# Feed-forward of a two-layer block in fp32: product and masked product stay in the PSUM bank of up, VectorE takes the low part from there, GpSimd only splits weights

## The chip, the cores and the metric

The kernel runs on one core of one Trainium2 chip. The metric is the device time of one execution in microseconds (us), lower is better. All times here are of that one core.

## The reference

The input x is 4 x 512 tokens of 128 numbers. It goes through two layers, each an alignment or attention step followed by a feed-forward. Only the feed-forwards matter here; each is a mixture of experts behind a layer norm.

```python
# layer 0: 64 experts of 64 hidden rows, 8 chosen for each token, and one shared expert
gate_out = jnp.einsum('bsh,ehi->bsei', hidden_states, expert_gate_k)
up_out = jnp.einsum('bsh,ehi->bsei', hidden_states, expert_up_k)
expert_act = jax.nn.silu(gate_out) * up_out
routed = jnp.einsum('bsei,eih->bsh', expert_act * router_mask[..., None], expert_down_k)
return shared + routed
...
# layer 1: 8 experts of 344 hidden rows, 2 chosen for each token, and one shared expert
for e in range(E):
    y = y + cw[:, e:e + 1] * _ffn(xf, wg[e], wu[e], wd[e])     # _ffn: silu(x wg') * (x wu') wd'
y = y + _ffn(x, swg, swu, swd)
```

router_mask and cw are zero for the experts that a token did not choose. The kernel computes all experts for all tokens and multiplies by the mask.

## The kernel before, in words

**Arithmetic.** A matmul in fp32r keeps fewer bits than fp32. So each factor is split into a high part (a copy rounded to fp32r) and a low part (the number less its high part), and a product is three matmuls into one PSUM bank: high x high, low weight x high, high weight x low (`three_pass`, L1010 to L1014).

**Tiling.** The hidden rows of all experts are cut into groups of 128: 33 in the first feed-forward, 25 in the second. The 2048 tokens are four chunks of 512. A group and a chunk are a unit: 132 units, then 100. `feed_forward(f)` stands in the program of each engine; f is 0 or 1, g the group, k the chunk, u = 4g + k the unit, i = k % 2 the buffer.

**One unit.**
- TensorE, `gate_up` (L1128): gate into bank 4 or 5, up into bank 6 or 7, three matmuls of 128x512 each (L1012 to L1014).
- ScalarE, `unit` (L836): silu of the bank of gate into act_s (L846).
- VectorE, `unit` (L1629): product act_t = act_s x bank of up (L1639), then the masked product act_a = act_t x mask (L1647).
- ScalarE, `hi` (L829): high part act_hi of act_a (L834).
- GpSimd, `unit` (L695): low part act_lo = act_a - act_hi (L700).
- TensorE, `down` (L1141): three matmuls into the bank of the chunk, 0 to 3 (L1144, L1145, L1147), which adds up over all groups.

**Order.** It is written by hand, with a semaphore for each step. TensorE does gate and up of unit u and then down of unit u-2; ScalarE silu of u, then the high part of u-1. Everything between is double buffered: act_s, act_t, act_a, act_hi, act_lo and the banks 4/5 and 6/7. The first three groups (PEEL) and the last two (REST) are unrolled; the rest is a loop over four groups (BODY).

**Waits around the change.** Gate of unit u waits for silu and for the product of unit u-2, which is what frees the bank of up:

```python
pe.wait_ge(FF[f]["silu"], u - 1)
pe.wait_ge(FF[f]["t"], u - 1)
```

The masked product waits for the low part of u-2 (the reader of act_a). The high part and the low part wait for down of u-2, which frees act_hi and act_lo.

**Weights.** SyncE loads w_raw a group ahead; ScalarE copies it to w_hi (L842) at chunk 2 of the group before; VectorE then makes w_lo (`split_lo`, L1623 to L1627). The splits of groups 0 and 1 are made earlier, by `first_lo`. Masks come by DMA from scr_mask, two for each group.

**Ends.** Before unit 2, TensorE starts the banks 0 to 3 with matmuls of one row of zeros (L1173). In the first units of the second feed-forward VectorE also does the routing of layer 1 (`route1`, L1468), in pieces ahead of units 0 to 3.

## Time and profile before

| | |
|---|---|
| runs | 926.32, 926.35, 929.34 us, median 926.35 |
| span of the profiled execution | 928.2 us |
| TensorE matmuls | 714.0 us busy, 77% |
| VectorE | 773.9 us busy, 83% |
| ScalarE | 432.5 us busy, 47% |
| GpSimd | 438.0 us busy, 47% |

The profile is of one execution. Its span runs from the first to the last instruction; what a run has around it is small, as the three runs lie from 1.9 us below that span to 1.1 us above it. In the rows, PE is TensorE's matmuls, PEld its weight loads, DVE VectorE, ACT ScalarE, POOL GpSimd. Names are those of the program without buffer numbers: "bank" is any PSUM bank, "arena" is the SBUF area that holds mask, act_s, act_t and act_a. L12 is line 12 of the kernel before. The records of two matmuls in a row overlap, so their starts tell the pace. Waits name the engine that waited and the last one that released it.

### The profile page before, as it was taken

To read this page: it belongs to the slowest core of one execution; us is meant where nothing else is said; L and a number is where in the kernel's file an instruction comes from. 1 tells how busy PE (TensorE), PEld (TensorE's weight loads), DVE (VectorE), ACT (ScalarE), POOL (GpSimd) and SP (SyncE) were. 2 spreads that over 40 slices of the span, in tenths; PEclk is the share of its full clock that TensorE was granted. 3 is DMA by queue.
4 is the path that set the end of the run, shared out by engine and by line. 5 is a ranking of instruction groups with operands and counts; after the bars stand their busy time and mean duration, and the time that the engine had idled before them with its cause. 6 is when DMAs were issued, how large, how long until landed. Compare 5 with 4: busy or idle time off the path is not lost.

```text
span 928.2 us, 13152 instructions
## 1 busy us (share of the span) xinstructions
PE 714.0 (77%) x3115; PEld 537.3 (58%) x3115; DVE 773.9 (83%) x1829; ACT 432.5 (47%) x757; POOL 438.0 (47%) x451
## 2 busy tenths in 40 slices
PE   3422200038999999999999978999999999999996
PEld 2211100036776676767667647998866767766674
DVE  6599569998899898989889887777697988989895
ACT  2344100024555555555555545444445555555553
POOL 5568600005655556565555652110136565555653
PEclk9655555555999999999999978999589999999999
DMA  4454650003676675757666400000327656455551
GB/s 122 78 127 137 146 65 0 0 9 75 147 146 124 131 137 124 140 113 146 121 136 132 116 1 9 1 0 0 72 53 147 145 114 147 117 142 127 129 131 46
DMA packets 84164, 89.44 MB, mean 96 GB/s; under 512 B 48958, under 2 KB 61859, under 8 KB 80609
## 3 DMA queue, kind: packets, MB, share of 16 engines
q1 hardware_dynamic: 79808, 79.38, 41.3%
q0 software_dynamic: 4320, 9.68, 3.7%
q8 instruction: 11, 0.18, 0.1%
q14 instruction: 25, 0.20, 0.1%
HBM read 79.84 MB, written 8.70 MB: 95 GB/s over the span
## 4 chain that ended last, share of the span: by engine, by line
DVE 27%; issue 27%; PE 25%; POOL 11%; ACT 5%; DMA 3%; SPq 1%; POOLq 1%; DVEq 0%
POOL act_lo L700 10%; DVE arena L1647 8%; DVE junk L1417 6%; PE bank L1012 4%; PE bank L1076 4%; PE bank L1014 4%; PE bank L1013 4%; ACT act_hi L834 3%; PE bank L1147 2%; PE bank L1058 2%; DVE arena L1374 2%; DVE arena L1383 1%; PE bank L948 1%; DVE arena L1639 1%; PE bank L1144 1%
## 5 line engine op out<-in xcount | busy, mean ns | idle before, releaser
L700 POOL TENSOR_TENSOR act_lo<-arena,act_hi 128x512 fp32r<-128x512 f32 x232 | 323.4, 1403 | 237.7 <-ACT act_hi L834 232.1
L1647 DVE TENSOR_TENSOR arena<-arena 128x512 f32<-128x512 f32 x232 | 311.2, 1341 | 22.1 <-POOL act_lo L700 12.3
L846 ACT ACTIVATE arena<-bank 128x512 f32<-128x512 f32 x232 | 138.9, 599 | 140.7 <-PE bank L1014 137.2
L834 ACT ACTIVATE act_hi<-arena 128x512 fp32r<-128x512 f32 x232 | 147.0, 633 | 94.2 <-PE bank L1147 51.0
L1012 PE MATMUL bank<-xn_hi,w_hi 128*128 128x512 f32 x464 | 188.4, 406 | 3.1 <-issue 1.9
L1639 DVE TENSOR_TENSOR arena<-arena,bank 128x512 f32<-128x512 f32 x232 | 157.8, 680 | 37.1 <-ACT arena L846 19.6
L1013 PE MATMUL bank<-xn_hi,w_lo 128*128 128x512 f32 x464 | 185.6, 400 | 0.0
L1014 PE MATMUL bank<-xn_lo,w_hi 128*128 128x512 f32 x464 | 185.6, 400 | 0.0
L1147 PE MATMUL bank<-act_lo,w_hi 128*128 128x512 f32 x232 | 104.1, 449 | 31.2 <-POOL act_lo L700 30.9
L1012 PEld LDWEIGHTS bank<-xn_hi,w_hi 128*128 128x128 f32 x464 | 88.7, 191 | 26.8 <-issue 7.2
L1014 PEld LDWEIGHTS bank<-xn_lo,w_hi 128*128 128x128 f32 x464 | 88.5, 191 | 21.1
L1013 PEld LDWEIGHTS bank<-xn_hi,w_lo 128*128 128x128 f32 x464 | 88.5, 191 | 18.9
L1144 PE MATMUL bank<-act_hi,w_hi 128*128 128x512 f32 x232 | 92.6, 399 | 0.0
L1145 PE MATMUL bank<-act_hi,w_lo 128*128 128x512 f32 x232 | 91.8, 396 | 0.0
L1147 PEld LDWEIGHTS bank<-act_lo,w_hi 128*128 128x128 f32 x232 | 43.6, 188 | 83.2 <-POOL act_lo L700 77.8
L602 POOL TENSOR_SCALAR xn<-x_res,mv,rstd 128x128 f32<-128x128 f32 x16 | 13.8, 866 | 135.9 <-DVE rstd L1307 106.8
L992 PE MATMUL bank<-ident,prep_in 128*128 128x128 f32 x75 | 22.1, 431 | 64.8 <-DMA prep_in<-in_L_ffn_wd 57.7
L1417 DVE TENSOR_SCALAR_CACHE_REDUCE junk<-arena,ecol 4x511 f16<-4x511 f16 x76 | 56.5, 744 | 8.3 <-DMA arena<-arena 5.6
L1000 PE MATMUL bank<-ident,ecol 128*77 128x128 f32 x1 | 0.5, 499 | 77.7 <-DVE junk L1417 77.7
L992 PEld LDWEIGHTS bank<-ident,prep_in 128*128 128x128 f32 x75 | 12.4, 210 | 74.3 <-DMA prep_in<-in_L_ffn_wd 69.5
L1144 PEld LDWEIGHTS bank<-act_hi,w_hi 128*128 128x128 f32 x232 | 43.6, 188 | 11.4 <-issue 0.7
L1145 PEld LDWEIGHTS bank<-act_hi,w_lo 128*128 128x128 f32 x232 | 43.8, 189 | 10.2
(199 smaller groups left out, 956.2 us busy)
## 6 DMA issues: line engine op xcount, KB each, us to landing
arena<-scr_mask SPq DMA_DIRECT2D x94, 512.0 KB, 6.2
scr_w<-prep_out POOLq DMA_DIRECT2D x25, 192.0 KB, 2.2
w_raw<-scr_w SPq DMA_DIRECT2D x25, 192.0 KB, 6.5
arena<-scr_one SPq DMA_DIRECT2D x6, 512.0 KB, 6.0
w_raw<-in_L_ffn_expert_gate_k SPq DMA_DIRECT2D x32, 64.0 KB, 6.1
w_raw<-in_L_ffn_expert_up_k SPq DMA_DIRECT2D x32, 64.0 KB, 5.8
w_raw<-in_L_ffn_expert_down_k SPq DMA_DIRECT2D x64, 32.0 KB, 5.4
prep_in<-in_L_ffn_wg POOLq DMA_DIRECT2D x21, 64.0 KB, 2.4
```

The costliest lines, as they stand in the source:

```text
L700: nc.gpsimd.tensor_tensor(act_lo[:, k % 2, :], act_a[:, k % 2, :], act_hi[:, k % 2, :].bitcast(F32), ALU.subtract).then_inc(FF[f]["alo"], 1)
L834: nc.scalar.activation(act_hi[:, j, :], act_a[:, j, :], ACT.Copy).then_inc(FF[f]["ahi"], 1)
L846: nc.scalar.activation(act_s[:, k % 2, :], ps[4 + k % 2][:], ACT.Silu).then_inc(FF[f]["silu"], 1)
L1012: nc.tensor.matmul(out, w_h, x_h, start=start, stop=False)
L1013: nc.tensor.matmul(out, w_l, x_h, start=False, stop=False)
L1014: return nc.tensor.matmul(out, w_h, x_l, start=False, stop=stop)
L1144: nc.tensor.matmul(ps[n][:], w_hi[:, j, DOWN:DOWN + P], act_hi[:, i, :], start=False, stop=False)
L1145: nc.tensor.matmul(ps[n][:], w_lo[:, j, DOWN:DOWN + P], act_hi[:, i, :], start=False, stop=False)
L1147: nc.tensor.matmul(ps[n][:], w_hi[:, j, DOWN:DOWN + P], act_lo[:, i, :], start=False, stop=False).then_inc(FF[f]["down"], 1)
L1417: nc.vector.tensor_scalar(junk[CHASE, 1:S], chase[:, i, 1:S], ecol[CHASE, i:i + 1], 0.0, ALU.is_le, ALU.add, accum_out=ecol[CHASE, i - 1:i ...
L1639: nc.vector.tensor_tensor(act_t[:, i, :], act_s[:, i, :], ps[6 + i][:], ALU.mult).then_inc(FF[f]["t"], 1)
L1647: nc.vector.tensor_tensor(act_a[:, i, :], act_t[:, i, :], mask[:, j, 512 * k:512 * (k + 1)], ALU.mult).then_inc(FF[f]["act"], 1)
```

## The change

- act_t and act_a are gone. VectorE writes the product back into the bank of up, and the masked product into the same bank again.
- ScalarE takes the high part from that bank.
- The low part moves from GpSimd to VectorE (`low_part`): it reads the bank and act_hi. In `unit` it comes after the masked product of unit u, for unit u-1.
- TensorE's wait for the product of u-2 ahead of gate is gone. Ahead of up stands a wait for the low part of u-2.
- The masked product and the high part no longer wait for the low part of u-2, nor the product for the masked product of u-2.
- GpSimd makes w_lo of the groups from 2 on in place of VectorE, as soon as w_hi is there.

```diff
--- before.py
+++ after.py
@@ -222,10 +222,8 @@
         mark[0] = 0
         mask = view([2, TOK])
         act_s = view([2, 512])
-        act_t = view([2, 512])
-        act_a = view([2, 512])
         yT = view([CHUNKS, 512])
-        mark[0] += FT * P
+        mark[0] += FT * P + 4 * 512
         XT_FROM = mark[0]
         xT = view([TOK])
         aff = [view([TILES, E]) for E in EXPERTS]
@@ -692,24 +690,19 @@
                 ins.then_inc(s_sel, 1)
 
             def feed_forward(f):
-                def unit(g, k):
-                    u = CHUNKS * g + k
-                    pool.wait_ge(FF[f]["ahi"], u + 1)
-                    if not (isinstance(g, int) and u < 2):
-                        pool.wait_ge(FF[f]["down"], u - 1)
-                    nc.gpsimd.tensor_tensor(act_lo[:, k % 2, :], act_a[:, k % 2, :], act_hi[:, k % 2, :].bitcast(F32),
-                                            ALU.subtract).then_inc(FF[f]["alo"], 1)
-
-                for u in range(CHUNKS * PEEL):
-                    if f == 0 and u == 0:
-                        for b in range(B):
-                            route0(b)
-                    unit(u // CHUNKS, u % CHUNKS)
-                with pool.Fori(0, LOOPS[f]) as t:
-                    for u in range(BODY * CHUNKS):
-                        unit(BODY * t + PEEL + u // CHUNKS, u % CHUNKS)
-                for u in range(CHUNKS * (GROUPS[f] - REST), CHUNKS * GROUPS[f]):
-                    unit(u // CHUNKS, u % CHUNKS)
+                def split_lo(g, j):
+
+                    pool.wait_ge(FF[f]["whi"], g + 1)
+                    nc.gpsimd.tensor_tensor(w_lo[:, j, :], w_raw[:, j, :], w_hi[:, j, :].bitcast(F32),
+                                            ALU.subtract).then_inc(FF[f]["wlo"], 1)
+
+                if f == 0:
+                    for b in range(B):
+                        route0(b)
+                split_lo(2, 0)
+                with pool.Fori(0, (GROUPS[f] - PEEL) // 2) as t:
+                    for jj in range(2):
+                        split_lo(2 * t + PEEL + jj, 1 - jj)
 
             norm(1)
             feed_forward(0)
@@ -829,9 +822,8 @@
                 def hi(u, j):
                     act.wait_ge(FF[f]["act"], u + 1)
                     if not (isinstance(u, int) and u < 2):
-                        act.wait_ge(FF[f]["alo"], u - 1)
                         act.wait_ge(FF[f]["down"], u - 1)
-                    nc.scalar.activation(act_hi[:, j, :], act_a[:, j, :], ACT.Copy).then_inc(FF[f]["ahi"], 1)
+                    nc.scalar.activation(act_hi[:, j, :], ps[6 + j][:], ACT.Copy).then_inc(FF[f]["ahi"], 1)
 
                 def unit(g, k, j, load=None):
                     u = CHUNKS * g + k
@@ -1131,10 +1123,11 @@
                         pe.wait_ge(FF[f]["wlo"], g + 1)
                     if not (isinstance(g, int) and u < 2):
                         pe.wait_ge(FF[f]["silu"], u - 1)
-                        pe.wait_ge(FF[f]["t"], u - 1)
                     tok = slice(512 * k, 512 * (k + 1))
                     three_pass(ps[4 + k % 2][:], w_hi[:, j, 0:P], w_lo[:, j, 0:P],
                                xn_hi[:, tok], xn_lo[:, tok]).then_inc(FF[f]["gate"], 1)
+                    if not (isinstance(g, int) and u < 2):
+                        pe.wait_ge(FF[f]["alo"], u - 1)
                     three_pass(ps[6 + k % 2][:], w_hi[:, j, UP:UP + P], w_lo[:, j, UP:UP + P],
                                xn_hi[:, tok], xn_lo[:, tok]).then_inc(FF[f]["up"], 1)
 
@@ -1172,6 +1165,8 @@
 
                     nc.tensor.matmul(ps[n][:], zeros[0:1, 0:P], zeros[0:1, :], start=True, stop=False)
                 for u in range(2, CHUNKS * PEEL):
+                    if u < CHUNKS:
+                        wait_low(pe, 2 * f + 1, u)
                     gate_up(u // CHUNKS, u % CHUNKS, u // CHUNKS % 2)
                     down(u - 2, (u - 2) % CHUNKS, (u - 2) // CHUNKS % 2)
                 with pe.Fori(0, LOOPS[f]) as t:
@@ -1193,7 +1188,7 @@
                     if n == 0:
                         pe.wait_ge(FF[f]["silu"], units)
                     if n == 2:
-                        pe.wait_ge(FF[f]["t"], units)
+                        pe.wait_ge(FF[f]["alo"], units)
                     pe.wait_ge(FF[f]["yT"], n + 1)
                     for q in range(4):
                         mm = nc.tensor.transpose(ps[4 + n][:, P * q:P * (q + 1)], yT[:, n, P * q:P * (q + 1)], ident[:])
@@ -1620,32 +1615,28 @@
                 route1(0, 0)
 
             def feed_forward(f):
-                def split_lo(g, j):
-
-                    dve.wait_ge(FF[f]["whi"], g + 1)
-                    nc.vector.tensor_tensor(w_lo[:, j, :], w_raw[:, j, :], w_hi[:, j, :].bitcast(F32),
-                                            ALU.subtract).then_inc(FF[f]["wlo"], 1)
-
-                def unit(g, k, j, half, last=False):
+                def low_part(u, i):
+                    dve.wait_ge(FF[f]["ahi"], u + 1)
+                    if not (isinstance(u, int) and u < 2):
+                        dve.wait_ge(FF[f]["down"], u - 1)
+                    nc.vector.tensor_tensor(act_lo[:, i, :], ps[6 + i][:], act_hi[:, i, :].bitcast(F32),
+                                            ALU.subtract).then_inc(FF[f]["alo"], 1)
+
+                def unit(g, k, j, half):
                     u = CHUNKS * g + k
                     i = k % 2
-                    early = isinstance(g, int) and u < 2
-                    if k == SPLIT_AT and not last and not (isinstance(g, int) and g == 0):
-                        split_lo(g + 1, 1 - j)
                     dve.wait_ge(FF[f]["silu"], u + 1)
                     dve.wait_ge(FF[f]["up"], u + 1)
-                    if not early:
-                        dve.wait_ge(FF[f]["act"], u - 1)
-                    nc.vector.tensor_tensor(act_t[:, i, :], act_s[:, i, :], ps[6 + i][:], ALU.mult).then_inc(FF[f]["t"], 1)
+                    nc.vector.tensor_tensor(ps[6 + i][:], act_s[:, i, :], ps[6 + i][:], ALU.mult).then_inc(FF[f]["t"], 1)
                     if f == 0 and isinstance(g, int) and g == 1:
                         dve.wait_ge(s_mask1[k], 16 * MASK_DMAS)
                     elif k == 0:
                         dve.wait_ge(FF_MASK[f][j], mask_loaded(f, half, j))
                     dve.wait_ge(FF[f]["t"], u + 1)
-                    if not early:
-                        dve.wait_ge(FF[f]["alo"], u - 1)
-                    nc.vector.tensor_tensor(act_a[:, i, :], act_t[:, i, :], mask[:, j, 512 * k:512 * (k + 1)],
+                    nc.vector.tensor_tensor(ps[6 + i][:], ps[6 + i][:], mask[:, j, 512 * k:512 * (k + 1)],
                                             ALU.mult).then_inc(FF[f]["act"], 1)
+                    if not (isinstance(g, int) and u < 1):
+                        low_part(u - 1, 1 - i)
 
                 for g in range(PEEL):
                     for k in range(CHUNKS):
@@ -1668,7 +1659,8 @@
                             unit(BODY * t + PEEL + i, k, (PEEL + i) % 2, BODY // 2 * t + (PEEL + i) // 2)
                 for g in range(GROUPS[f] - REST, GROUPS[f]):
                     for k in range(CHUNKS):
-                        unit(g, k, g % 2, g // 2, last=g == GROUPS[f] - 1)
+                        unit(g, k, g % 2, g // 2)
+                low_part(CHUNKS * GROUPS[f] - 1, 1)
 
             first_lo(0)
             norm(1, add_aligned)
```

TensorE in a unit of the first feed-forward (unit 6), before: gate, up, down of unit u-2.

```order
L1012 MATMUL bank<-xn_hi,w_hi 128x512 [waits ff0_t,ff0_silu]
L1013 MATMUL bank<-xn_hi,w_lo 128x512
L1014 MATMUL bank<-xn_lo,w_hi 128x512
L1012 MATMUL bank<-xn_hi,w_hi 128x512
L1013 MATMUL bank<-xn_hi,w_lo 128x512
L1014 MATMUL bank<-xn_lo,w_hi 128x512
L1144 MATMUL bank<-act_hi,w_hi 128x512 [waits ff0_ahi]
L1145 MATMUL bank<-act_hi,w_lo 128x512
L1147 MATMUL bank<-act_lo,w_hi 128x512 [waits ff0_alo]
```

The same unit after:

```order
L1004 MATMUL bank<-xn_hi,w_hi 128x512 [waits ff0_silu]
L1005 MATMUL bank<-xn_hi,w_lo 128x512
L1006 MATMUL bank<-xn_lo,w_hi 128x512
L1004 MATMUL bank<-xn_hi,w_hi 128x512 [waits ff0_alo]
L1005 MATMUL bank<-xn_hi,w_lo 128x512
L1006 MATMUL bank<-xn_lo,w_hi 128x512
L1137 MATMUL bank<-act_hi,w_hi 128x512 [waits ff0_ahi]
L1138 MATMUL bank<-act_hi,w_lo 128x512
L1140 MATMUL bank<-act_lo,w_hi 128x512 [waits ff0_alo]
```

The wait for the product ("t") ahead of gate is gone, and ahead of the first matmul of up stands one for a low part ("alo"), which no longer comes from GpSimd but from VectorE.

VectorE in two units of group 2 of the first feed-forward, before ("arena" is act_s, act_t, act_a and the mask):

```order
L1639 TENSOR_TENSOR arena<-arena,bank 128x512 [waits ff0_act,ff0_up,ff0_silu]
L1647 TENSOR_TENSOR arena<-arena 128x512 [waits ff0_alo,ff0_t,ff0_mask_loaded0]
L1639 TENSOR_TENSOR arena<-arena,bank 128x512 [waits ff0_act,ff0_up,ff0_silu]
L1647 TENSOR_TENSOR arena<-arena 128x512 [waits ff0_alo,ff0_t]
L1626 TENSOR_TENSOR w_lo<-w_raw,w_hi 128x384 [waits ff0_whi]
```

The same two units after:

```order
L1630 TENSOR_TENSOR bank<-arena,bank 128x512 [waits ff0_up,ff0_silu]
L1636 TENSOR_TENSOR bank<-bank,arena 128x512 [waits ff0_t,ff0_mask_loaded0]
L1622 TENSOR_TENSOR act_lo<-bank,act_hi 128x512 [waits ff0_down,ff0_ahi]
L1630 TENSOR_TENSOR bank<-arena,bank 128x512 [waits ff0_up,ff0_silu]
L1636 TENSOR_TENSOR bank<-bank,arena 128x512 [waits ff0_t]
L1622 TENSOR_TENSOR act_lo<-bank,act_hi 128x512 [waits ff0_down,ff0_ahi]
```

Each unit has three operations in place of two, the split of the weights (L1626) has left, and every third row is the low part of the unit before, ahead of the next product.

## Rows read from the trace of the kernel before

**Rows 1.** The page, part 5: line, engine, names | busy us, mean ns | idle, releaser

```profile
L700 POOL TENSOR_TENSOR act_lo<-arena,act_hi 128x512 fp32r<-128x512 f32 x232 | 323.4, 1403 | 237.7 <-ACT act_hi L834 232.1
L1647 DVE TENSOR_TENSOR arena<-arena 128x512 f32<-128x512 f32 x232 | 311.2, 1341 | 22.1 <-POOL act_lo L700 12.3
L834 ACT ACTIVATE act_hi<-arena 128x512 fp32r<-128x512 f32 x232 | 147.0, 633 | 94.2 <-PE bank L1147 51.0
L1639 DVE TENSOR_TENSOR arena<-arena,bank 128x512 f32<-128x512 f32 x232 | 157.8, 680 | 37.1 <-ACT arena L846 19.6
```

**Rows 2.** Timeline, VectorE: start us, us, engine, line, names [idle, releaser]

```profile
232.29 0.69 DVE L1647 TENSOR_TENSOR arena<-arena 128x512 f32<-128x512 f32 x1
...
538.07 1.68 DVE L1647 TENSOR_TENSOR arena<-arena 128x512 f32<-128x512 f32 x1
...
685.62 0.69 DVE L1647 TENSOR_TENSOR arena<-arena 128x512 f32<-128x512 f32 x1
686.85 0.65 DVE L1639 TENSOR_TENSOR arena<-arena,bank 128x512 f32<-128x512 f32 x1
687.54 1.34 DVE L1647 TENSOR_TENSOR arena<-arena 128x512 f32<-128x512 f32 x1
...
915.20 1.69 DVE L1647 TENSOR_TENSOR arena<-arena 128x512 f32<-128x512 f32 x1
```

**Rows 3.** Windows: stretch, its us, busy us of each engine, clock, DMA

```profile
core 0: us, PE busy (x) PEld busy (x) DVE busy (x) ACT busy (x) POOL busy (x), PEclk, DMA share, GB/s
300.00:500.00 200.00, 188.39 (x757) 138.81 (x758) 179.32 (x190) 112.83 (x189) 116.61 (x84) 1.00 0.65 131
```

**Rows 4.** Waits, 300 to 500 us: waiter, releaser, us in total, times, longest

```profile
PEld bank L1147 <- POOL act_lo L700: 28.2, 43, 1.1
...
ACT act_hi L834 <- PE bank L1147: 21.0, 21, 1.0
```

**Rows 5.** Timeline, TensorE, 455 us, after a stop

```profile
455.12 0.50 PE L1147 MATMUL bank<-act_lo,w_hi 128*128 128x512 f32 x1 [0.58 <-POOL act_lo L700]
...
455.46 0.39 PE L1012 MATMUL bank<-xn_hi,w_hi 128*128 128x512 f32 x1
...
455.69 0.39 PE L1013 MATMUL bank<-xn_hi,w_lo 128*128 128x512 f32 x1
```

**Rows 6.** Groups by form, VectorE, 128x512 out of a bank and out of SBUF

```profile
L1259 DVE TENSOR_TENSOR xn_lo<-arena,xn_hi 128x512 fp32r<-128x512 f32 x8 | 5.4, 676 | 2.4 <-ACT xn_hi L748 2.4
...
L1271 DVE SCALAR_TENSOR_TENSOR arena<-bank,bias,arena 128x512 fp32r<-128x512 f32 x4 | 3.0, 751 | 2.4 <-ACT arena L753 2.3
...
L1259 DVE TENSOR_TENSOR xn_lo<-bank,xn_hi 128x512 fp32r<-128x512 f32 x4 | 2.8, 692 | 3.9 <-ACT arena L743 3.9
```

**Rows 7.** Timeline, all engines, 441 to 450 us

```profile
441.24 1.29 POOL L700 TENSOR_TENSOR act_lo<-arena,act_hi 128x512 fp32r<-128x512 f32 x1 [1.29 <-ACT act_hi L834]
...
442.57 0.19 PEld L1147 LDWEIGHTS bank<-act_lo,w_hi 128*128 128x128 f32 x1 [0.38 <-POOL act_lo L700]
...
447.10 0.40 PE L1014 MATMUL bank<-xn_lo,w_hi 128*128 128x512 f32 x1
...
447.59 0.69 DVE L1639 TENSOR_TENSOR arena<-arena,bank 128x512 f32<-128x512 f32 x1 [0.24 <-PE bank L1014]
...
448.31 1.70 DVE L1647 TENSOR_TENSOR arena<-arena 128x512 f32<-128x512 f32 x1
...
449.94 0.55 DVE L1626 TENSOR_TENSOR w_lo<-w_raw,w_hi 128x384 fp32r<-128x384 f32 x1
```

**Rows 8.** Windows, as rows 3, at both levels of the clock

```profile
700.60:704.00 3.40, 2.36 (x11) 1.52 (x10) 3.35 (x4) 2.16 (x4) 1.95 (x2) 1.00 1.01 205
226.10:229.50 3.40, 2.55 (x10) 1.70 (x10) 2.97 (x15) 0.38 (x1) 2.63 (x5) 0.99 0.39 81
229.60:233.00 3.40, 3.26 (x8) 2.00 (x7) 3.31 (x5) 1.28 (x3) 1.87 (x2) 0.51 0.52 127
```

**Rows 9.** Timeline, TensorE, 226 us

```profile
226.26 1.19 PE L1173 MATMUL bank<-zeros 1*128 1x512 f32 x4
```

## The prediction

> **What bounds the kernel now.** I read the page's list of costliest groups first [rows 1]. The two feed-forwards work in units (512 tokens of one group of 128 hidden rows); there are 132 in the first and 100 in the second, 232 in all, and every group of the unit has x232. The dearest are GpSimd's low part (L700, 1.40 us) and VectorE's masked product (L1647, 1.34 us); the product that comes before it (L1639) takes 0.68 us, though both go over 128x512 numbers. Then I took the length of a unit from the starts of the masked products [rows 2]: units 2 to 131 of the first feed-forward start at 232.29 and 538.07, which is 305.78 / 129 = 2.37 us a unit; units 3 to 99 of the second at 687.54 and 915.20, 227.66 / 96 = 2.37 us. So the 228 units of the steady stretches hold some 540 us of the span of 928.2.
>
> The view by windows tells who fills that time [rows 3]: from 300 to 500 us TensorE shows 188.39 of 200 us busy, VectorE 179.32, at full clock. TensorE's records overlap, so I take the spacing of two matmuls in a row, 455.46 and 455.69, which is 0.23 us [rows 5]; nine matmuls a unit are 2.09 us. TensorE therefore works 2.09 of 2.37 us. What ends its waits in that stretch is one thing, the low part of GpSimd (28.2 us); the high part on ScalarE, ahead of it, waits in turn for the third matmul of down (21.0 us), which frees the buffers [rows 4]. No single wait dominates: the loop is loose, with 0.28 us a unit of slack on TensorE, some 64 us in all. That is what a better order could win.
>
> **The change, part by part.** *Removed:* 232 low parts on GpSimd and 54 splits of weights on VectorE (0.56 us each, a quarter of it a unit, 0.14 us). GpSimd keeps only the splits, one in four units, which the work of four units hides on any reading. *VectorE's work:* product 0.68, masked product, low part. Of its two inputs the masked product now has one in PSUM, as the product has (0.68 us on average over 232 units with GpSimd at work beside it), so I take 0.69 for it in place of 1.34. The low part has an operation of the same form in the trace, xn_lo<-bank,xn_hi, 0.69 us [rows 6]. Back to back that is about 0.72 + 0.62 + 0.62 = 1.96 us a unit, against 0.68 + 1.34 + 0.14 = 2.16 before. By busy time the change is a gain, and neither VectorE (1.96) nor TensorE (2.09) would need 2.37 us.
>
> The row that the two forms of xn_lo give, 0.676 us with both inputs in SBUF and 0.692 with one in PSUM, puts the price of an input from PSUM at 0.016 us [rows 6]. The Trainium skill has it higher: "VectorE: DVE Perf Modes", in the section on the TRN2 errata, gives VectorE a fixed part of 120 cycles for a source in PSUM and 58 for one in SBUF, 62 cycles more, an estimate of 0.065 us at 0.96 GHz. By the page masked product and low part would each be dearer by that, and the time 228 x 0.13 = 30 us over my sum; the trace decides for the row.
>
> *The added waits.* What matters is what waits for whom. Product and masked product used to leave the bank of up at once: its next writer, up of unit u, waited for the product of unit u-2 ("t"), long done. Now the value stays in the bank until the low part has read it, so up of unit u waits for "alo" of unit u-2. The low part of unit u-2 stands on VectorE behind product and masked product of unit u-1 (the order of VectorE in the section on the change), and that product waits for up of unit u-1. So there is a closed loop through **every** unit: up(u-1), product(u-1), masked product(u-1), low part(u-2), up(u). Nothing in it overlaps anything else in it. On TensorE, down(u-3) and gate(u) stand between up(u-1) and up(u), 6 x 0.23 = 1.4 us, and are done before the low part is; behind the waiting up(u) are down(u-2) and gate(u+1), which wait with it.
>
> The loop, from the first matmul of up after a stop:
> - first to third matmul: 455.12 to 455.69, 0.57 us (a restart shows 0.34 to the second, then 0.23) [rows 5];
> - the third runs 0.40; the product starts 0.09 after its end (447.10 + 0.40 to 447.59) [rows 7];
> - product to masked product, which waits for it: 447.59 to 448.31, 0.72 [rows 7];
> - masked product to low part, which does not wait for it: 0.69 less the overlap that 448.31 + 1.70 against 449.94 shows, 0.07, so 0.62 [rows 7]. Its other waits, the high part and down, are fulfilled by then;
> - low part 0.69 [rows 6], and 0.04 until TensorE starts (441.24 + 1.29 to 442.57, there from GpSimd) [rows 7].
>
> Sum: 0.57 + 0.40 + 0.09 + 0.72 + 0.62 + 0.69 + 0.04 = **3.13 us a unit**, where it was 2.37. VectorE then works 1.96 us of 3.13 and TensorE 2.09, and both wait for each other in turn. ScalarE (the high part takes 0.63 [rows 1], silu of the same size about as much, and a weight copy comes each fourth unit) fits: silu of a unit starts with the end of gate, well ahead of up, and the high part only has to be there when VectorE comes to the low part a unit later. The masks have more time to land than before. GpSimd, at 1 to 2 us each fourth unit, does too.
>
> *The sum.* First feed-forward: 129 x 3.13 = 403.8 against 305.8, +98.0. Second: 96 x 3.13 = 300.5 against 227.7, +72.8. At the starts the first up that waits for a low part comes late by some 1.8 us in the first (high part and low part of unit 0 now stand ahead of up of unit 2), and by 3.13 less 685.62 to 687.54 = 1.2 in the second [rows 2], where the routing steps on VectorE cover the first units: +3.0. At each end the last masked product is shorter (1.69 to 0.69) [rows 2] and the last low part too (about 1.29, as the one at 441.24 [rows 7], to 0.69): -1.6 twice, -3.2. Together +170.6, so a span of 928.2 + 170.6 = 1098.8. The three runs lie between 1.9 us below that span and 1.1 above it, so I carry the difference to their median: 926.35 + 170.6 = **1097 us**, slower by 18%.
>
> *Bounds of what is not shown.* No VectorE operation of the trace writes PSUM. Below: every one of the three saves 0.03 (a short product takes 0.65, at 686.85 [rows 2]) and the starts save 0.05 by a direct wait: 2.99, 228 x -0.14 = -32, 1065 us. Above: all three cost what the dearest 128x512 operation out of a bank costs, 0.75 [rows 6]: 3.33, +46, 1143 us. I take the middle rows because two of the three forms stand in the trace almost as they are.
>
> **Rival 1: the loop is no bound, TensorE is (faster).** If the low part were ready when TensorE comes to up, the unit would fall to nine matmuls, 2.09 us, and the kernel to 926.35 - 228 x 0.28 = 862 us. For it: the busy sums above, all under 2.37; two 1.3 us operations that run against each other are gone. It decides at 2.37 us a unit: the loop would have to be shorter by 0.76, so the three VectorE operations by 0.25 each, to 0.44. No 128x512 operation on two fp32 inputs in [rows 1, 6] is under 0.67 on average. The Trainium skill speaks for this rival: "SBUF — State Buffer", Who interferes with whom, says that a VectorE instruction with two SBUF inputs contends with a GpSimd instruction that reads SBUF, and one with a single SBUF input does not. The trace agrees (1.34 against 0.68), but that relief lies off the loop that the new wait makes. Chance 0.03.
>
> **Rival 2: the clock falls in the gaps.** TensorE will stand still about 0.9 us in every unit. At half clock its matmuls come every 3.4 / 8 = 0.43 us, as 229.6 to 233.0 shows at 0.51 of full clock [rows 8], so nine take 3.83, more than the loop. All the way that is 228 x 1.46 = +333, 1259 us; for half of the time 1178. For it: 226.1 to 229.5, with 2.55 of 3.40 us busy and ten matmuls, was followed by the stretch at half clock [rows 8]. Against: four of those ten were the short row of zeros on one partition (L1173) [rows 9]; 700.6 to 704.0, eleven matmuls and 2.36 us busy, stayed at 1.00 [rows 8]. The changed kernel has 9 x 3.4 / 3.13 = 9.8 full matmuls in such a stretch and no gap over 1 us. The Trainium skill warns of it in "TensorE: Matmul & The Clock Gate", A second HAM failure mode: short idles between groups of matmuls at each turn of the banks can make the clock swing. No row of this trace shows that for full matmuls. Chance 0.06.
>
> **Rival 3: VectorE is slow on PSUM.** If writing a bank, or reading back what was just written there, costs over 0.2 us more a unit than my upper rows, the kernel passes 1143 us: with 0.25 us more on each of the two writes, 3.63 a unit, it is 1211 us. Nothing in the trace speaks for it, nothing excludes it. Chance 0.05.
>
> **How the numbers follow.** The forecast with its bounds, 0.86, 1065 to 1143; the rest are the rivals. The range takes in the bounds of the unknown prices and nothing of the rivals, which hold 0.14. A measurement of this kernel can tell some 0.5%, about 5 us, from no change. Slower by more: forecast and rivals 2 and 3, 0.96 with a little taken off for a loop that I drew wrongly; the same 0.01; faster 0.03.
>
> **What would show it.** Right: masked products start every 3.1 us; the largest wait of the stretch is TensorE at the first matmul of up for the low part on VectorE, near 0.9 us, 228 times; VectorE waits for the third matmul of up, near 1.1 us, each unit; masked product 0.69; GpSimd nearly idle; granted clock 1.00. Wrong: a wait of TensorE under 0.3 us (rival 1), a clock under 1.00 in the steady stretch (rival 2), VectorE operations over 0.8 us (rival 3).

## The result, and the profile after

The changed kernel takes 1108.85 us (median of 4 runs, 1108.71 to 1110.34), the kernel before 926.48 us (926.32 to 929.34). The ratio is 1.196, with a 95% interval of 1.193 to 1.198: slower by 182.4 us. Forecast were 1097 us and a range of 1065 to 1143.

The page of the changed kernel, the costliest groups (columns as in [rows 1]); product, masked product and low part are now L1630, L1636 and L1622, the first matmul of gate and of up is L1004, silu L838, the high part L826, GpSimd's split of weights L696:

```profile
PE 743.2 (67%) x3115; PEld 529.4 (48%) x3115; DVE 746.7 (67%) x2007; ACT 404.5 (37%) x757; POOL 167.9 (15%) x273
...
L1004 PE MATMUL bank<-xn_hi,w_hi 128*128 128x512 f32 x464 | 210.4, 453 | 186.7 <-DVE act_lo L1622 186.7
L1630 DVE TENSOR_TENSOR bank<-arena,bank 128x512 f32<-128x512 f32 x232 | 161.4, 696 | 258.1 <-PE bank L1006 258.1
...
L1636 DVE TENSOR_TENSOR bank<-bank,arena 128x512 f32<-128x512 f32 x232 | 162.3, 699 | 12.2
L1622 DVE TENSOR_TENSOR act_lo<-bank,act_hi 128x512 fp32r<-128x512 f32 x232 | 157.9, 681 | 0.1
L696 POOL TENSOR_TENSOR w_lo<-w_raw,w_hi 128x384 fp32r<-128x384 f32 x54 | 53.9, 997 | 648.6 <-ACT w_hi L834 648.6
```

Against [rows 1], every edit did by itself what it was meant to. The masked product fell from 1.341 us to 0.699, the low part from 1.403 on GpSimd to 0.681 on VectorE. VectorE's busy time fell too, from 773.9 us to 746.7, although it took over 232 low parts. What grew is idle time: TensorE stands 186.7 us at the first matmul of up for VectorE's low part, VectorE 258.1 us at the product for the third matmul of up. The two wait for each other in turn.

The same in the steady stretch, by window (columns as in [rows 3], where TensorE had 188.39 us and 757 matmuls, and VectorE 179.32), and the waits there (as [rows 4]):

```profile
300.00:500.00 200.00, 148.57 (x568) 101.52 (x567) 124.78 (x190) 76.79 (x142) 15.95 (x16) 1.00 0.50 100
```

```profile
PEld bank L1004 <- DVE act_lo L1622: 79.0, 63, 1.6
...
DVE bank L1630 <- PE bank L1006: 71.9, 63, 1.5
...
PE bank L1004 <- DVE act_lo L1622: 51.4, 63, 1.1
```

In place of the several small waits of [rows 4] there is one pair, once in each of the 63 units of the stretch: 0.8 us of TensorE, 1.1 us of VectorE. One turn of the loop on the timeline (start us, us, engine, line, names, idle before and who ended it):

```profile
399.72 0.50 PE L1004 MATMUL bank<-xn_hi,w_hi 128*128 128x512 f32 x1 [0.78 <-DVE act_lo L1622]
...
400.30 0.40 PE L1006 MATMUL bank<-xn_lo,w_hi 128*128 128x512 f32 x1
...
400.80 0.70 DVE L1630 TENSOR_TENSOR bank<-arena,bank 128x512 f32<-128x512 f32 x1 [1.14 <-PE bank L1006]
...
401.53 0.70 DVE L1636 TENSOR_TENSOR bank<-bank,arena 128x512 f32<-128x512 f32 x1
...
402.14 0.68 DVE L1622 TENSOR_TENSOR act_lo<-bank,act_hi 128x512 fp32r<-128x512 f32 x1
...
402.88 0.50 PE L1004 MATMUL bank<-xn_hi,w_hi 128*128 128x512 f32 x1 [0.79 <-DVE act_lo L1622]
```

From one first matmul of up to the next it is 402.88 - 399.72 = 3.16 us, and the steps follow one another without a gap: 1.08 to the product, 0.73 to the masked product, 0.61 to the low part, 0.74 to the next up.

### The profile page after: what moved, and what is told of

It is laid out like the page before. It is cut to its first block, busy times and chain, and to the rows that moved or that the text cites. A ratio compares the mean times of both kernels' runs of the same rounds, so it can differ in the third digit from the quotient of the medians.

```text
span 1107.1 us, 12511 instructions
## 1 busy us (share of the span) xinstructions
PE 743.2 (67%) x3115; PEld 529.4 (48%) x3115; DVE 746.7 (67%) x2007; ACT 404.5 (37%) x757; POOL 167.9 (15%) x273
## 4 chain that ended last, share of the span: by engine, by line
DVE 46%; PE 32%; issue 16%; DMA 2%; DVEq 2%; ACT 1%; SPq 1%; POOL 0%
DVE bank L1630 15%; DVE act_lo L1622 14%; PE bank L1004 11%; PE bank L1006 6%; PE bank L1005 6%; DVE junk L1412 5%; PE bank L1068 3%; PE bank L1050 2%; DVE bank L1636 1%; DVE arena L1369 1%; DVE arena L1378 1%; PE bank L940 1%; DVEq L1628 1%; DVE arena L1377 1%; DMA arena<-scr_d 1%
## 5 line engine op out<-in xcount | busy, mean ns | idle before, releaser
L1004 PE MATMUL bank<-xn_hi,w_hi 128*128 128x512 f32 x464 | 210.4, 453 | 186.7 <-DVE act_lo L1622 186.7
L1630 DVE TENSOR_TENSOR bank<-arena,bank 128x512 f32<-128x512 f32 x232 | 161.4, 696 | 258.1 <-PE bank L1006 258.1
L838 ACT ACTIVATE arena<-bank 128x512 f32<-128x512 f32 x232 | 138.5, 597 | 371.4 <-PE bank L1006 369.1
L1004 PEld LDWEIGHTS bank<-xn_hi,w_hi 128*128 128x128 f32 x464 | 88.3, 190 | 297.2 <-DVE act_lo L1622 286.1
L1636 DVE TENSOR_TENSOR bank<-bank,arena 128x512 f32<-128x512 f32 x232 | 162.3, 699 | 12.2
L1622 DVE TENSOR_TENSOR act_lo<-bank,act_hi 128x512 fp32r<-128x512 f32 x232 | 157.9, 681 | 0.1
L696 POOL TENSOR_TENSOR w_lo<-w_raw,w_hi 128x384 fp32r<-128x384 f32 x54 | 53.9, 997 | 648.6 <-ACT w_hi L834 648.6
L826 ACT ACTIVATE act_hi<-bank 128x512 fp32r<-128x512 f32 x232 | 137.5, 592 | 8.7 <-DVE bank L1636 8.7
L1140 PE MATMUL bank<-act_lo,w_hi 128*128 128x512 f32 x232 | 92.4, 398 | 0.3 <-DVE act_lo L1622 0.3
L834 ACT ACTIVATE w_hi<-w_raw 128x384 fp32r<-128x384 f32 x54 | 28.3, 525 | 79.4 <-PE bank L1140 79.4
```

Source lines behind the costliest of these rows:

```text
L826: nc.scalar.activation(act_hi[:, j, :], ps[6 + j][:], ACT.Copy).then_inc(FF[f]["ahi"], 1)
L838: nc.scalar.activation(act_s[:, k % 2, :], ps[4 + k % 2][:], ACT.Silu).then_inc(FF[f]["silu"], 1)
L1004: nc.tensor.matmul(out, w_h, x_h, start=start, stop=False)
L1140: nc.tensor.matmul(ps[n][:], w_hi[:, j, DOWN:DOWN + P], act_lo[:, i, :], start=False, stop=False).then_inc(FF[f]["down"], 1)
L1622: nc.vector.tensor_tensor(act_lo[:, i, :], ps[6 + i][:], act_hi[:, i, :].bitcast(F32), ALU.subtract).then_inc(FF[f]["alo"], 1)
L1630: nc.vector.tensor_tensor(ps[6 + i][:], act_s[:, i, :], ps[6 + i][:], ALU.mult).then_inc(FF[f]["t"], 1)
```

## Experiments

Three theories went in. **A**, that of the prediction: the new wait closes a loop up, product, masked product, low part, up, and nothing in it overlaps. **B**: the work that VectorE took over is too much for it. **C**: operations that write PSUM, or read back what was just written there, are what is slow. The unit's length is taken as in the prediction, from the starts of masked products; it is 3.18 us in the first feed-forward of the changed kernel. A ratio is to the kernel before, which was run again beside each set of experiments (medians 927.75 to 928.61 us).

### The same operations, the low part one place earlier

The low part of the unit before goes between product and masked product. The masked product then stands behind the low part for which up waits, not ahead of it.

```diff
                     nc.vector.tensor_tensor(ps[6 + i][:], act_s[:, i, :], ps[6 + i][:], ALU.mult).then_inc(FF[f]["t"], 1)
+                    if not (isinstance(g, int) and u < 1):
+                        low_part(u - 1, 1 - i)
...
-                    if not (isinstance(g, int) and u < 1):
-                        low_part(u - 1, 1 - i)
```

> The changed kernel with one call moved: on VectorE the low part of unit u-1 stands between product and masked product of unit u, no longer behind both. Same instructions, same waits, same banks. Theory A, the closed loop up, product, masked product, low part, up: the masked product leaves the loop. From the changed kernel's rows: first matmul of up to product 1.08, product to low part 0.62 (no wait between them), low part 0.68, 0.06 to the next up: 2.44 us a unit in place of 3.17, so 1109 - 228 x 0.73 = 943 us. Theory B, VectorE carries too much work (three operations and PSUM for both inputs and outputs): the work is the same, so 1109 us, or at most 1090 for the wait between product and masked product that is now covered.

Measured: 939.49 us (937.98 to 940.97), 1.011 of the kernel before (1.009 to 1.013); 2.44 us a unit. One call at another place gives back 169 of the 182 us. VectorE's timeline:

```profile
399.58 0.70 DVE L1630 TENSOR_TENSOR bank<-arena,bank 128x512 f32<-128x512 f32 x1 [0.52 <-PE bank L1006]
400.19 0.68 DVE L1622 TENSOR_TENSOR act_lo<-bank,act_hi 128x512 fp32r<-128x512 f32 x1
400.79 0.69 DVE L1638 TENSOR_TENSOR bank<-bank,arena 128x512 f32<-128x512 f32 x1
402.00 0.69 DVE L1630 TENSOR_TENSOR bank<-arena,bank 128x512 f32<-128x512 f32 x1 [0.52 <-PE bank L1006]
```

Product to product is 2.42 us: 0.61 to the low part, and from there 1.81 over the next up to the next product. The masked product, 0.69 us, now runs while TensorE begins up. The operations have the lengths that they had, so B and C can't explain the 182 us; A does.

### The low part ahead of the product

The same call moved up once more, ahead of the product of unit u.

```diff
                     i = k % 2
+                    if not (isinstance(g, int) and u < 1):
+                        low_part(u - 1, 1 - i)
                     dve.wait_ge(FF[f]["silu"], u + 1)
...
-                    if not (isinstance(g, int) and u < 1):
-                        low_part(u - 1, 1 - i)
```

> The changed kernel with the low part of unit u-1 ahead of the product of unit u. Theory A: up no longer waits behind the low part's predecessors, but VectorE now waits for the high part of the unit that it has just masked: product 0.73, masked product 0.70 and 0.04 to ScalarE, high part 0.59 and 0.04 back, low part 0.61 to the next product: 2.71 us a unit, 1109 - 228 x 0.46 = 1004 us, and TensorE's wait for the low part is gone. Theory B: the same work on VectorE, 1109 us.

Measured: 1015.59 us (1014.66 to 1016.67), 1.094 (1.092 to 1.096); 2.77 us a unit. TensorE's wait for the low part stays, 60.9 us at its weight load in 300 to 500 us (72 times), where I had expected it gone. The forecast of 1004 came near the time; the reading of the waits was half right. ScalarE and VectorE on the timeline:

```profile
401.95 0.70 DVE L1638 TENSOR_TENSOR bank<-bank,arena 128x512 f32<-128x512 f32 x1
...
402.76 0.60 ACT L826 ACTIVATE act_hi<-bank 128x512 fp32r<-128x512 f32 x1 [1.01 <-DVE bank L1638]
...
403.48 0.69 DVE L1622 TENSOR_TENSOR act_lo<-bank,act_hi 128x512 fp32r<-128x512 f32 x1 [0.83 <-ACT act_hi L826]
...
404.09 0.68 DVE L1632 TENSOR_TENSOR bank<-arena,bank 128x512 f32<-128x512 f32 x1
404.88 0.70 DVE L1638 TENSOR_TENSOR bank<-bank,arena 128x512 f32<-128x512 f32 x1
```

Masked product, high part, low part and the next product now follow one another through ScalarE: 0.81 + 0.72 + 0.61, and 0.79 to the next masked product, 2.93 us here; over the four units of a group it is 2.69, 2.69, 2.93 and 2.78. That is another closed loop, again of the order alone. TensorE's wait is its consequence: the low part comes late because its high part does.

### Less of the loop's work, and less of the work beside it

Two cuts that leave out part of the computation, each in one place. The first shortens the masked product, which A has in the loop; the second takes a matmul of down away, which A has beside it.

```diff
-                    nc.vector.tensor_tensor(ps[6 + i][:], ps[6 + i][:], mask[:, j, 512 * k:512 * (k + 1)],
+                    nc.vector.tensor_tensor(ps[6 + i][:, 0:32], ps[6 + i][:, 0:32], mask[:, j, 512 * k:512 * k + 32],
```

> The changed kernel with the masked product over 32 of its 512 columns (the other 480 stay unmasked). It takes 0.49 us out of the operation (512 columns take 0.68, 384 take 0.55, so 1.0 ns a column). Theory A: the masked product lies in the closed loop, so every unit gets shorter by all of it: 228 x 0.49 = 112 us, 997 us. If something else bounded the unit (TensorE at 2.09, the clock), the time would fall by less or not at all.

Measured: 995.07 us (993.21 and 996.92), 2.69 us a unit. In the steady stretch the operation took 199 ns in place of 699, 0.50 us less, and the unit became 0.49 us shorter: one to one.

```diff
                     nc.tensor.matmul(ps[n][:], w_hi[:, j, DOWN:DOWN + P], act_hi[:, i, :], start=False, stop=False)
-                    nc.tensor.matmul(ps[n][:], w_lo[:, j, DOWN:DOWN + P], act_hi[:, i, :], start=False, stop=False)
```

> The changed kernel without the middle matmul of down (low weight x high part is left out), eight matmuls a unit in place of nine. Theory A: down lies beside the loop, TensorE only waits longer (about 1.0 us in place of 0.8): 1109 us, and the granted clock stays 1.00 in the steady stretch, or the gaps do matter and it falls. If TensorE's work counted: 228 x 0.23 = 53 us less, 1056 us.

Measured: 1108.16 us (1108.10 and 1108.23), 3.18 us a unit: nothing, with 0.23 us less of TensorE's work in each of 232 units. The window, and the wait that took it up:

```profile
300.00:500.00 200.00, 133.90 (x505) 89.73 (x504) 124.83 (x190) 76.90 (x142) 15.96 (x16) 1.00 0.49 100
```

```profile
PE bank L1004 <- DVE act_lo L1621: 66.1, 63, 1.4
```

TensorE waits 66.1 us where it waited 51.4. The stretch also bears on rival 2: TensorE stood still for 1.05 us in each unit and its granted clock stayed at 1.00, that is at 2.4 GHz.

### Product and masked product in SBUF, all else as changed

act_t and act_a come back as buffers; up waits for the product of u-2 ("t"), which reads the bank last. High part and low part read act_a (lines not shown). The low part stays on VectorE at its place after the masked product, the splits stay on GpSimd. Against the changed kernel this takes away the bank hold; with it three operations change the place of their operands, and product and masked product wait for the readers of act_t and act_a again.

```diff
-                        pe.wait_ge(FF[f]["alo"], u - 1)
+                        pe.wait_ge(FF[f]["t"], u - 1)
...
-                    nc.vector.tensor_tensor(ps[6 + i][:], act_s[:, i, :], ps[6 + i][:], ALU.mult).then_inc(FF[f]["t"], 1)
+                    if not (isinstance(g, int) and u < 2):
+                        dve.wait_ge(FF[f]["act"], u - 1)
+                    nc.vector.tensor_tensor(act_t[:, i, :], act_s[:, i, :], ps[6 + i][:], ALU.mult).then_inc(FF[f]["t"], 1)
...
-                    nc.vector.tensor_tensor(ps[6 + i][:], ps[6 + i][:], mask[:, j, 512 * k:512 * (k + 1)],
+                    if not (isinstance(g, int) and u < 2):
+                        dve.wait_ge(FF[f]["alo"], u - 1)
+                    nc.vector.tensor_tensor(act_a[:, i, :], act_t[:, i, :], mask[:, j, 512 * k:512 * (k + 1)],
```

> The changed kernel with the banks set free as before the change: the product goes to act_t and the masked product to act_a in SBUF, and up waits for the product of u-2 in place of its low part. The low part stays on VectorE behind the masked product of the next unit, GpSimd only splits weights. Theory A: the loop is cut; what is left goes through the third matmul of down and holds two units: 1.08 + 0.73 + 0.61 + 0.74 + 1.03 (third matmul of down to first of up) = 4.19, 2.10 a unit, about TensorE's nine matmuls, 2.09. 2.12 a unit gives 1109 - 228 x 1.05 = 870 us, faster than the kernel before the change. Theory B, VectorE's load: three operations as in the changed kernel, 1109 us. Theory C, the operations are slow because they use PSUM: their rows fall, the time falls only by that, some 0.02 each, to 1095.

Measured: 890.30 us (888.42 to 893.51), 0.959 (0.956 to 0.961); 2.22 us a unit. So the bank hold, with this order, costs 1108.85 - 890.30 = 218.6 us (a little more by itself, as the low part is dearer in SBUF, below), and the rest of the change gains. VectorE does the same three operations, which settles B: it is busy 187.15 of 200 us in 300 to 500 us and the kernel is faster than before. It is 20 us above what I expected, and the page shows where:

```profile
L1624 DVE TENSOR_TENSOR act_lo<-arena,act_hi 128x512 fp32r<-128x512 f32 x232 | 183.4, 791 | 0.2
```

The low part, with both inputs in SBUF, takes 0.791 us on average in place of 0.681. One low part in four meets a split on GpSimd, and the timeline shows both orders:

```profile
399.12 0.69 DVE L1624 TENSOR_TENSOR act_lo<-arena,act_hi 128x512 fp32r<-128x512 f32 x1
399.16 1.52 POOL L698 TENSOR_TENSOR w_lo<-w_raw,w_hi 128x384 fp32r<-128x384 f32 x1 [8.32 <-ACT w_hi L836]
...
407.48 1.03 POOL L698 TENSOR_TENSOR w_lo<-w_raw,w_hi 128x384 fp32r<-128x384 f32 x1 [6.80 <-ACT w_hi L836]
407.55 1.51 DVE L1624 TENSOR_TENSOR act_lo<-arena,act_hi 128x512 fp32r<-128x512 f32 x1
```

Whichever starts second is the longer by about what is left of the first: the split by 0.52 us with 0.65 left of the low part, the low part by 0.82 with 0.96 left of the split. So about half of the meetings, one low part in eight (12 of 91 in 300 to 500 us), lengthen the low part. Out of a bank it is not lengthened. The changed kernel:

```profile
408.39 0.99 POOL L696 TENSOR_TENSOR w_lo<-w_raw,w_hi 128x384 fp32r<-128x384 f32 x1 [11.59 <-ACT w_hi L834]
...
408.51 0.68 DVE L1622 TENSOR_TENSOR act_lo<-bank,act_hi 128x512 fp32r<-128x512 f32 x1
```

The Trainium skill says this in "SBUF — State Buffer", Who interferes with whom: a VectorE instruction with two SBUF inputs contends with a GpSimd instruction that reads SBUF, one with a single SBUF input does not, and the order of issue decides who blocks. The trace agrees on all three.

### The same with the low part between

The order that gained most in the bank, tried with the SBUF buffers.

```diff
                     nc.vector.tensor_tensor(act_t[:, i, :], act_s[:, i, :], ps[6 + i][:], ALU.mult).then_inc(FF[f]["t"], 1)
+                    if not (isinstance(g, int) and u < 1):
+                        low_part(u - 1, 1 - i)
...
-                    if not (isinstance(g, int) and u < 1):
-                        low_part(u - 1, 1 - i)
```

> The same as the run with act_t and act_a in SBUF, and the low part of u-1 between product and masked product of u. Theory A: no loop over TensorE and VectorE is near 2.09 any more (two units: 4.19 - 0.73 = 3.5), VectorE does about 1.9 a unit, TensorE's nine matmuls bound the unit: 2.09 to 2.12, 863 to 870 us. Against the run before it this shows whether the loop through down still costs something: if it does, this one is faster by up to 10 us. Theory B: 1109.

Measured: 894.75 us (894.00 to 895.70), 0.963 (0.962 to 0.965). That is 4 us slower than the other order, where I expected up to 10 us of gain. The masked product is now the one that a split meets (1.51 us at 397.03, 1.50 at 406.00, mean 887 ns in 300 to 500 us), and ScalarE waits 66.3 us for it there with the high part. Where up waits only for the product, there is no loop for this order to cut.

### The splits taken by themselves

First on the kernel before: its splits go to GpSimd, in the order of the low parts, behind the low part of the third unit of each group. Nothing else changes.

```diff
                     unit(u // CHUNKS, u % CHUNKS)
+                    if u >= CHUNKS and u % CHUNKS == SPLIT_AT:
+                        split_lo(u // CHUNKS + 1, (u // CHUNKS + 1) % 2)
...
-                    if k == SPLIT_AT and not last and not (isinstance(g, int) and g == 0):
-                        split_lo(g + 1, 1 - j)
```

> The kernel before the change with one part of it alone: GpSimd splits the weights of groups 2 on, ahead of the low part two units on, and VectorE no longer does. The low part stays on GpSimd, the masked product in SBUF. VectorE saves 0.14 us a unit, GpSimd gets 1.0 to 1.1 us more each fourth unit, ahead of a low part for which TensorE waits already (28 us of 200). If GpSimd is what bounds the loose loop of before: 0.1 to 0.25 us a unit more, 228 x 0.17 = 39 us, about 965 us. If VectorE did: 228 x 0.14 = 32 us less, 895 us.

Measured: 1106.69 us (1106.45 to 1107.38), 1.192 (1.189 to 1.196), against some 965 expected: my largest miss. GpSimd and TensorE on the timeline, then the window:

```profile
397.26 1.70 POOL L706 TENSOR_TENSOR act_lo<-arena,act_hi 128x512 fp32r<-128x512 f32 x1 [1.29 <-ACT act_hi L846]
398.93 0.99 POOL L698 TENSOR_TENSOR w_lo<-w_raw,w_hi 128x384 fp32r<-128x384 f32 x1
```

```profile
400.15 0.47 PE L1024 MATMUL bank<-xn_hi,w_hi 128*128 128x512 f32 x1 [3.47 <-POOL w_lo L698]
...
402.07 0.63 PE L1157 MATMUL bank<-act_hi,w_lo 128*128 128x512 f32 x1
402.50 0.63 PE L1159 MATMUL bank<-act_lo,w_hi 128*128 128x512 f32 x1
```

```profile
300.00:500.00 200.00, 154.50 (x554) 117.24 (x553) 118.47 (x123) 79.45 (x139) 102.59 (x76) 0.89 0.47 95
```

The low part of a group's third unit waited for a high part (1.29 us); the split behind it waited along; gate of the next group waited for the split; and TensorE does that gate ahead of down of two units before. So TensorE stood still once a group, 3.47 us here and 2.3 to 3.5 us in other groups. After 11 of the 13 stops between 300 and 470 us it did seven or eight matmuls 0.43 us apart, an estimated 1.6 us more than at 0.23, and the clock of the stretch is 0.89. I had priced the split's time and not its place in GpSimd's queue.

With the split two places earlier, ahead of the low part of the second unit:

```diff
+                    if u >= CHUNKS and u % CHUNKS == 1:
+                        split_lo(u // CHUNKS + 1, (u // CHUNKS + 1) % 2)
                     unit(u // CHUNKS, u % CHUNKS)
...
-                    if k == SPLIT_AT and not last and not (isinstance(g, int) and g == 0):
-                        split_lo(g + 1, 1 - j)
```

> Again the kernel before the change with the splits of the weights on GpSimd alone, but the split stands ahead of the low part of the second unit of a group, not behind that of the third. In the first try w_lo came 3.5 us late in every group (TensorE idle 3.47 us at the first gate, then matmuls 0.43 us apart at half clock), since the split was queued behind a low part that itself comes two units after VectorE's work. If place was the cause, that wait is gone: GpSimd has 1.40 + 0.25 us of work a unit under 2.37, TensorE waits a little more for the low part once in four units, 0 to 0.25 us a unit, 925 to 985 us, 945 likeliest. If GpSimd cannot take the split beside the low part at all, it stays over 1000 us.

Measured: 937.56 us (935.41 to 940.46), 1.012 (1.008 to 1.015). The stop is gone, clock 1.00, and what is left of the move is a loss of 1.2%. The likely reason, not tested further, is that GpSimd, for whose low part TensorE waits in both kernels, has the more to do (139.56 us busy of 200, 116.61 in [rows 3]).

Then the other half, the low part alone: product and masked product in SBUF, low part on VectorE, splits on VectorE as before. It differs from the SBUF kernel above in this only, where `split_lo` went back from GpSimd:

```diff
-                    pool.wait_ge(FF[f]["whi"], g + 1)
-                    nc.gpsimd.tensor_tensor(w_lo[:, j, :], w_raw[:, j, :], w_hi[:, j, :].bitcast(F32),
+                    dve.wait_ge(FF[f]["whi"], g + 1)
+                    nc.vector.tensor_tensor(w_lo[:, j, :], w_raw[:, j, :], w_hi[:, j, :].bitcast(F32),
```

> The run with act_t and act_a in SBUF and the low part on VectorE behind the masked product, but with the splits of the weights on VectorE too, as before the change, so that GpSimd has no work in the units. There each fourth low part of VectorE ran 1.51 us in place of 0.68 while GpSimd's split was at work, and the unit was 2.217 us where I had worked out 2.12. If that collision is what is missing: VectorE gets 0.12 us a unit of splits but loses the collisions (0.2), is at 2.06, TensorE at 2.09: 2.12 a unit, 890 - 228 x 0.10 = 867 us. If VectorE's load is the bound instead: 890 us or more.

Measured: 879.51 us (878.80 to 880.26), 0.948 (0.945 to 0.950). So the move of the low part, with the waits that go or change place along with it, is worth 48 us, and the splits on GpSimd take 11 us of it back, by the collisions above. With GpSimd idle in the units, the masked product takes 0.693 us where it took 1.341 beside GpSimd's low parts [rows 1], and the low part 0.685 where it took 1.403. What the waits by themselves are worth was not tried.

### The split on GpSimd in three pieces

If the second comer is held by what is left of the first, shorter GpSimd instructions hold it less.

```diff
-                    nc.gpsimd.tensor_tensor(w_lo[:, j, :], w_raw[:, j, :], w_hi[:, j, :].bitcast(F32),
-                                            ALU.subtract).then_inc(FF[f]["wlo"], 1)
+                    for m in range(3):
+                        cols = slice(P * m, P * (m + 1))
+                        part = nc.gpsimd.tensor_tensor(w_lo[:, j, cols], w_raw[:, j, cols], w_hi[:, j, cols].bitcast(F32),
+                                                       ALU.subtract)
+                    part.then_inc(FF[f]["wlo"], 1)
```

> The run with act_t and act_a in SBUF (low part on VectorE, splits on GpSimd, 2.217 us a unit, 890 us), with each split of 128x384 cut into three of 128x128. There VectorE's low part ran 1.51 us beside GpSimd's 1.03 us. If VectorE is held until the GpSimd instruction ends, a shorter one holds it for less: 0.3 in place of 0.8 us once in four units, 2.10 to 2.15 a unit, 875 us; if the two share the port turn by turn, or if the three hold it three times, nothing is won: 890 us or a little more.

Measured: 874.50 us (873.72 to 875.18), 0.942 (0.940 to 0.945), the fastest of all, 53 us under the kernel before. Timeline and window:

```profile
402.71 1.76 POOL L700 TENSOR_TENSOR w_lo<-w_raw,w_hi 128x128 fp32r<-128x128 f32 x3 [6.56 <-ACT w_hi L839]
402.78 0.95 DVE L1627 TENSOR_TENSOR act_lo<-arena,act_hi 128x512 fp32r<-128x512 f32 x1
```

```profile
300.00:500.00 200.00, 200.00 (x845) 154.89 (x844) 187.32 (x282) 117.42 (x212) 42.89 (x72) 1.00 0.72 147
```

The low part that meets a split takes 0.95 us in place of 1.51. TensorE's records leave no gap in 200 us; 2.15 us a unit in the first feed-forward and 2.17 in the second is close to its nine matmuls at 0.23.

## Why the prediction was right, step by step

**The bound before.** The 0.28 us of slack a unit that [rows 2, 5] gave was real: the best version took 0.2 of it.

**The closed loop.** Shown. It is the only thing changed by moving the low part one place (-0.74 us a unit); 0.50 us taken out of it came back as 0.49; 0.23 us of work beside it came back as nothing; without the bank hold it is gone, at 2.22 us. The signs that the prediction named came true, but for one word: TensorE's wait is not the largest of the stretch. ScalarE waits longer, 99.2 us, but off the loop.

**The terms of the loop.** First matmul of up to product 1.08 (forecast 0.57 + 0.40 + 0.09 = 1.06), to masked product 0.73 (0.72), to low part 0.61 (0.62), to up 0.74 (0.73): 3.16 where I had 3.13. On top of that, units at chunk 0, where the masked product also waits for the mask, have 0.80 in the second step, the same 0.07 more in each group, which speaks against masks that landed late:

```profile
403.95 0.70 DVE L1630 TENSOR_TENSOR bank<-arena,bank 128x512 f32<-128x512 f32 x1 [1.13 <-PE bank L1006]
404.75 0.70 DVE L1636 TENSOR_TENSOR bank<-bank,arena 128x512 f32<-128x512 f32 x1
```

And once in 16 units, at the turn of the unrolled loop, a unit takes 3.27 us or more. The kernel before waits for the same masks and has the same unrolled loop, but has slack; in a closed loop nothing covers such a step. Together the unit was (642.87 - 232.85) / 129 = 3.18 us in the first feed-forward and (1097.14 - 793.12) / 96 = 3.17 in the second, on these starts of masked products:

```profile
232.85 0.70 DVE L1636 TENSOR_TENSOR bank<-bank,arena 128x512 f32<-128x512 f32 x1
...
642.87 0.70 DVE L1636 TENSOR_TENSOR bank<-bank,arena 128x512 f32<-128x512 f32 x1
...
793.12 0.70 DVE L1636 TENSOR_TENSOR bank<-bank,arena 128x512 f32<-128x512 f32 x1
...
1097.14 0.70 DVE L1636 TENSOR_TENSOR bank<-bank,arena 128x512 f32<-128x512 f32 x1
```

That is +104.2 and +76.4 us on [rows 2], 180.6 where the sum had 98.0 + 72.8 = 170.8. This term, 0.04 to 0.05 us a unit, is the larger part of the miss of 12 us: the forecast had no term for the wait for the mask or for the turn of the loop.

**Starts and ends.** Forecast +3.0 and -3.2. The first masked product that I counted came 0.56 us later than before, not 1.8; from the last unit of the first feed-forward to unit 3 of the second it took 0.78 us more, where I had -0.4; from the last masked product to the end of the span 3.0 us less, not 1.6. Each of the three was off by more than 1 us, and that they came to -1.7 in all where I had -0.2 is luck. The span grew by 178.9.

**Span to median.** Every run of the changed kernel is 1.7 to 1.8 us above its span. So is every run of the kernel before that was made beside the experiments (926.24 to 924.5, 930.88 to 929.1). By that the profiled execution of the kernel before took some 930 us, an estimate, 3.6 above its median, so the sum made against its span comes out that much too low when it is carried to the median. With it the miss of 12 us is accounted for: 9.8 from the units, 3.6 from this, less 1.5 at the starts and ends.

**Bounds.** 2.99 to 3.33 us a unit held 3.17. Writing a bank costs next to nothing: the product took 0.696 (0.684 into SBUF in the fastest version), the masked product 0.699 (0.693 in SBUF beside an idle GpSimd), the low part 0.681 out of a bank (0.685 out of SBUF). The Trainium skill ("VectorE: DVE Perf Modes", TRN2 errata) has a fixed part for a source in PSUM that would make an estimated 0.065 us, or 30 us in all; it does not appear on these operations, and the measurement decides: the row for xn_lo [rows 6] was the better guide.

**Rival 1, TensorE the bound.** Not here: 148.57 us busy of 200. Its relief was real, the masked product at 0.70 us in place of 1.34, but it did not lie off the loop, as the prediction says there. The masked product is a step of the loop, and 0.50 us less of it came back as 0.49. That reading was wrong and did no harm, since the sum had the step in the loop, at 0.69: the loop is 3.17 us with the relief. In SBUF, with the same work on VectorE, TensorE became the bound (2.15 us a unit in the fastest version).

**Rival 2, the clock.** Not here. The windows of the changed kernel:

```profile
231.20:234.60 3.40, 3.40 (x10) 2.49 (x9) 1.99 (x3) 0.00 (x0) 0.00 (x0) 0.50 0.42 112
...
238.00:651.00 413.00, 306.72 (x1176) 208.83 (x1174) 259.58 (x411) 158.61 (x293) 31.31 (x32) 1.00 0.46 94
...
791.00:1105.00 314.00, 234.07 (x898) 159.23 (x896) 196.93 (x298) 120.17 (x222) 22.96 (x23) 1.00 0.42 93
```

A piece at half clock stands at the start of the feed-forward, as in [rows 8]; the steady stretches are at full clock with TensorE still for 0.8 us in each unit.

**Rival 3, PSUM slow.** Not here: 0.696, 0.699 and 0.681 us, where the prediction took 0.68, 0.69 and 0.69.

## What to carry to other kernels

When a buffer is to be held longer, write down, for each engine, what stands between the operation that fills it and the one that frees it, and follow it round: a loop that returns to its start once per unit has the sum of its latencies as its period, whatever the busy times say. With the same operations, such a loop may be opened by one place in the order of one engine. Of a step moved to another queue, ask first what stands ahead of it there and who waits for it, and only then how long it takes.

## What the runs showed of the hardware that I had not expected

- A VectorE operation and a GpSimd operation that both read SBUF twice do not slow each other evenly: the second to start is held, whichever it is. The low part of 0.69 us took 1.51 when it started 0.07 us after a split of 1.03, and 0.95 when the split was in three pieces; the split took 1.52 when it started 0.04 after a low part. Three pieces cost GpSimd more (162 at 0.621 us, 96.6 us busy, against 54 at 1.256, 67.8 us), and VectorE less.
- Stops of 2.3 to 3.5 us, one in each group of some 13 us, brought the clock of the steady stretch to 0.89; stops of 0.8 to 1.05 us, one in each unit of 3.17, left it at 1.00. What lies between was not tried.
- Whether the bank hold can be had at 2.1 us a unit was not tried. With the low part between product and masked product the loop of up, product and low part, 1.08 + 0.61 + 0.73 = 2.42 us, is still there, and the unit was 2.44.
